# Attention passes with one row gather per tile of edges into a ring, rows copied per unit by SyncE, and a resident table of node blocks addressed by TensorE

## The reference

```python
def gatv2_layer(x, src, dst, Wl, Wr, att, bias, n_nodes, heads):
    xl = (x @ Wl).reshape(N, heads, Dh)
    xr = (x @ Wr).reshape(N, heads, Dh)
    e = leaky_relu(xl[src] + xr[dst], 0.2)
    logits = einsum('ehd,hd->eh', e, att)
    m = segment_max(logits, dst)
    a = exp(logits - m[dst])
    alpha = a / segment_sum(a, dst)[dst]
    out = segment_sum(alpha[:, :, None] * xl[src], dst)
    return out.mean(axis=1) + bias

# edges and self loops; L0 is two such layers with a relu between
x = layernorm(x + L0(x))
# L1: h = x + segment_sum(x[src], dst), then three dense layers
x = layernorm(x + L1(x))
```

## Time and profile before

| | us |
|---|---|
| runs (3) | 4044.29, 4044.32, 4049.66 |
| median | 4044.32 |
| span of the profiled execution | 4048.7 |
| layer 1 pass, first to last chunk start | about 200 to 1738 |
| layer 2 pass, first to last chunk start | 2095 to 3416 |
| TensorE busy | 3293.6 (81%) |
| VectorE busy | 2807.3 (69%) |
| GpSimd busy | 2796.9 (69%) |
| ScalarE busy | 1717.6 (42%) |

### The profile page before, as it was taken

The page is one execution under the profiler, slowest core; times in us unless marked ns, Lnnn a source line. Parts: engine busy times, 40 slices in busy tenths (PEclk is TensorE's granted clock), DMA queues, the critical chain, the costliest instruction groups (busy, mean ns, idle before and its releaser), DMA issues. The chain is left out here.

```text
span 4048.7 us, 76266 instructions
## 1 busy us (share of the span) xinstructions
PE 3293.6 (81%) x24199; PEld 2204.4 (54%) x24199; DVE 2807.3 (69%) x6887; ACT 1717.6 (42%) x3696; POOL 2796.9 (69%) x2157
## 2 busy tenths in 40 slices
PE   0399999999999999996339977777777777568986
PEld 0246666666666666674226655554455555346763
DVE  3558888888888888886537755565555555579972
ACT  3254444444444444432215433333333333147861
POOL 4488888888777777505678888888888885537630
PEclk9999999999999999986669988888888888569997
DMA  2233343343333333323114433333333332211210
GB/s 58 51 65 80 86 88 86 86 89 85 80 87 86 86 85 88 75 54 83 48 36 79 91 74 67 68 69 67 67 68 73 69 68 48 52 26 40 44 34 28
DMA packets 607173, 274.68 MB, mean 68 GB/s; under 512 B 445801, under 2 KB 568077, under 8 KB 606260
## 3 DMA queue, kind: packets, MB, share of 16 engines
q1 hardware_dynamic: 261848, 102.14, 11.7%
q0 software_dynamic: 107328, 77.78, 11.1%
q10 hardware_dynamic: 237600, 89.88, 9.1%
HBM read 161.25 MB, written 105.94 MB: 66 GB/s over the span
## 5 line engine op out<-in xcount | busy, mean ns | idle before, releaser
L901 PE MATMUL L_e_ps_z<-L_e_xT,L_w_abs 128*128 128x500 f32 x2700 | 1501.4, 642 | 0.0
L826 POOL DMA_INDIRECT L_e_xs<-in_x_dram,src_idx x880 | 1193.1, 1356 | 335.4 <-issue 261.4
L826 POOL DMA_INDIRECT L_e_xs<-x_d,src_idx x820 | 1079.7, 1317 | 253.3 <-issue 249.8
L952 PEld LDWEIGHTS L_e_ps_v<-L_e_xs,L_e_p 125*128 125x128 f32 x5400 | 860.0, 204 | 628.3 <-issue 569.6
L996 ACT ACTIVATE L_e_rl<-L_e_ps_z 128x500 f32<-128x500 f32 x1350 | 793.0, 587 | 883.0 <-PE L_e_ps_z L901 883.0
L952 PE MATMUL L_e_ps_v<-L_e_xs,L_e_p 125*128 125x65 f32 x5400 | 796.2, 274 | 11.1 <-DVE L_e_acc L1180 9.4
L1180 DVE SCALAR_TENSOR_TENSOR L_e_acc<-L_e_acc,L_e_row,L_e_ps_v 128x130 f32<-128x130 f32 (+1 forms) x1440 | 448.5, 311 | 424.1 <-PE L_e_ps_v L952 281.4
L888 PE MATMUL L_e_ps_x<-ident,L_e_xs 125*64 125x125 f32 x1800 | 288.7, 285 | 310.7 <-DMA L_e_xs<-x_d,src_idx 251.8
L989 ACT ACTIVATE L_e_xT<-L_e_ps_x 128x500 f32<-128x500 f32 x450 | 264.3, 587 | 619.3 <-PE L_e_ps_x L891 590.4
L901 PEld LDWEIGHTS L_e_ps_z<-L_e_xT,L_w_abs 128*128 128x128 f32 x2700 | 427.4, 198 | 77.8 <-issue 24.3
L1163 DVE TENSOR_TENSOR L_e_p<-L_e_ohc,L_e_ae 125x640 f32<-125x640 f32 x540 | 427.1, 818 | 0.0
(11 more groups left out here) (304 smaller groups left out, 3620.2 us busy)
## 6 DMA issues: line engine op xcount, KB each, us to landing
L_v_d<-L_e_acc ACTq DMA_DIRECT2D x225, 260.0 KB
L_e_dlb<-dloc_d SPq DMA_DIRECT2D x90, 468.8 KB, 4.9
L_v_d<-L_e_acc ACTq DMA_DIRECT2D x225, 130.0 KB
L_e_xw<-x_d SPq DMA_DIRECT2D x1800, 12.0 KB
L_e_xs<-in_x_dram,src_idx POOLq DMA_INDIRECT x900
L_e_xs<-x_d,src_idx POOLq DMA_INDIRECT x900
L_e_lim<-limits_d SPq DMA_DIRECT2D x180, 39.1 KB
L_max_d<-L_e_me SPq DMA_DIRECT2D x45, 78.1 KB
```

The source lines that it names most:

```text
L826: pool.indirect_dma_start(xs[c.slot(XR)][:, n, 0:D], None, lay.x_rows, bass.IndirectOffsetOnAxis(k.src_idx[:, u:u + 1], 0)).then_inc(gath[ ...
L901: pe.matmul(ps_z[part % ZR][:, 0:QT], lay.w_abs[:, part * 128:(part + 1) * 128], xT[q][:], start=True, stop=True).then_inc(s["z_ready"], 1)
L952: ins = pe.matmul(ps_v[u // 2 % 2][:, u % 2 * VX + v * XW:u % 2 * VX + (v + 1) * XW], p[st % 3][:, u % NQ, v, :, :].rearrange("e n h -> e ...
```

## The change

**Gathers.** GpSimd gathers each tile once (800 instead of 900 gathers a pass) into a ring `L_e_tiles` of TR = 64 tiles, in groups of TF = 16 (`fetch_tiles`). After a group has landed it adds one to `fetched_to`. Before a group is fetched over an old one, it waits until the chunks that use the old tiles are copied (`copied`, with a count read from `reuse`).

**Rows.** For each chunk SyncE runs `serve`: it waits for the chunk's list, signals `listed`, waits for the copies of the chunk before and signals `copied`, loads 20 ring places into registers with one load, waits until `fetched_to` has reached the chunk's last tile, and issues 20 copies from the ring to `L_e_xs` (now a ring of XR = 6 in both layers) inside SBUF. The list has three rows: window, place in the ring, group needed.

**Windows.** The rows of all 98 windows are loaded once per layer into SBUF. TensorE itself loads the four window addresses of the next step into registers at the end of each step (`window_blocks`) and uses them as the address of the weights. These weights are 128 columns wide, the second 64 being the window; partitions 0 to 63 of the result are overwritten by the transposes, which now come second.

**Rings.** The rings of `dlb` and of the limits have 2 places instead of 3 in layer 1. **Ahead.** Chunks served and groups fetched before the pass are 1 and 2 in layer 1, 3 and 4 in layer 2. **Setup.** Seven of nine gathers of source indices go; the indices per tile are transposed by TensorE; two more lists are stored to HBM.

The diff, cut to its core:

```diff
+TR = 64
+TF = 16
+NF = G // TF
+RF = TR // TF
+XR = 6
+LR = 8
+SERVED = (1, 3)
+FETCHED = (2, 4)
...
                 for b in range(NB):
...
+                    if b < 2:
+                        pool.indirect_dma_start(srcu[:, b * T:(b + 1) * T], None, a["src"].rearrange("(g e) -> g e", e=T),
+                                                bass.IndirectOffsetOnAxis(gidx[:, b:b + 1], 0)).then_inc(s["gather"], 16)
...
+                us = Dma(sp, s["unit_store"])
+                sp.wait_ge(s["units"], 4)
+                us.start(k.unit_d[1].rearrange("(b p) -> p b", p=BLK), ring_off[:], elements=True)
+                us.start(k.unit_d[2].rearrange("(b p) -> p b", p=BLK), need_i[:], elements=True)
+                us.wait()
...
-def fetch_rows(k, pool, lay, u0, u1):
-
-    for u in range(u0, u1):
-        pool.indirect_dma_start(lay.xs[u // CU][:, u % CU, 0:D], None, lay.x_rows,
-                                bass.IndirectOffsetOnAxis(k.src_idx[:, u:u + 1], 0)).then_inc(lay.gath[u // CU], 16)
...
-def load_windows(k, sp, lay, c):
-
-    for n in range(CU):
-        window = k.nc.values_load(lay.wins[c.slot(2)][0:1, n:n + 1], engines=[mybir.EngineType.SP], min_val=0, max_val=NW - 1,
-                                  skip_runtime_bounds_check_because="win_idx is the least of a count's rest and NW - 1")
-        sp.dma_start(lay.xw[c.slot(3)][:, n, :], bass.AP(k.x3_d.tensor, window * (WN * S3),
-                                                         [[D, 3 * WN], [1, D]])).then_inc(lay.ld_x[c.slot(3)], 16)
+def counts(eng, name, places):
+
+    regs = [eng.alloc_register(f"{name}{n}") for n in range(places.shape[1])]
+    eng.load(regs, places)
+    return [(eng.snap(r, donate=True, min_val=0, max_val=63) & 63) + 1 for r in regs]
+
+
+def fetch_tiles(k, pool, lay, f0, f1):
+
+    for f in range(f0, f1):
+        if f >= RF:
+            if (f - RF) % 16 == 0:
+                copies = counts(pool, f"{lay.nm}reuse{f}_", k.reuse[0:1, f - RF:min(f + 16, f1) - RF])
+            pool.wait_ge(lay.copied, copies[(f - RF) % 16])
+            pool.sem_inc(lay.freed, 1)
+        for i in range(TF):
+            g = f * TF + i
+            pool.indirect_dma_start(lay.tiles[:, g % TR * D:(g % TR + 1) * D], None, lay.x_rows,
+                                    bass.IndirectOffsetOnAxis(k.src_tile[:, g:g + 1], 0)).then_inc(lay.gath[f % RF], 16)
+            if i == 3 and f > f0:
+                tiles_there(pool, lay, f - 1)
+    tiles_there(pool, lay, f1 - 1)
+
+
+def tiles_there(pool, lay, f):
+
+    pool.wait_ge(lay.gath[f % RF], 16 * TF * (f // RF + 1))
+    pool.sem_inc(lay.fetched_to, 1)
+
+
+def list_units(k, sp, lay, c):
+
+    sp.dma_start(lay.lists[c.slot(LR)][:], bass.AP(k.unit_d.tensor, c.val(CU), [[3 * UT, 1], [UT, 3], [1, CU]])).then_inc(lay.ld_w[c.slot(2)], 16)
+
+
+def listed(eng, lay, c, row, start, step, top):
+
+    regs = [eng.alloc_register(f"{lay.nm}{row}_{c.number}_{n}") for n in range(start, CU, step)]
+    eng.load(regs, lay.lists[c.slot(LR)][0:1, row, start:CU:step])
+    return [eng.snap(r, donate=True, min_val=0, max_val=top) for r in regs]
+
+
+def rows_there(sp, lay, c):
+
+    sp.wait_ge(lay.ld_r[c.slot(XR)], c.uses(XR) * 16 * CU)
+    sp.sem_inc(lay.copied, 1)
+
+
+def load_rows(k, sp, lay, c):
+
+    places = listed(sp, lay, c, 1, 0, 1, (TR - 1) * D)
+    sp.wait_ge(lay.fetched_to, counts(sp, f"{lay.nm}need{c.number}_", lay.lists[c.slot(LR)][0:1, 2, CU - 1:CU])[0])
+    for n, at in enumerate(places):
+        sp.dma_start(lay.xs[c.slot(XR)][:, n, 0:D], lay.tiles[:, bass.ds(at, D)]).then_inc(lay.ld_r[c.slot(XR)], 16)
+
+
+def serve(k, sp, lay, c):
+
+    sp.wait_ge(lay.ld_w[c.slot(2)], c.uses(2) * 16)
+    sp.sem_inc(lay.listed, 1)
+    if c.after(1):
+        rows_there(sp, lay, c.back(1))
+    load_rows(k, sp, lay, c)
+    if c.back(-1).there():
+        list_units(k, sp, lay, c.back(-1))
...
+                sp.dma_start(lay.xw[:, 128 - D:].rearrange("r (w d) -> r w d", d=D),
+                             bass.AP(k.x3_d.tensor, 0, [[D, 3 * WN], [WN * S3, NW], [1, D]])).then_inc(lay.ld_x, 16)
+                serve(k, sp, lay, fixed(0))
...
-                fetch_rows(k, pool, lay, 0, EARLY if lay.norm else lay.ahead * CU)
+                pool.memset(lay.xw[:, 0:128 - D], 0.0).then_inc(s["ones"], 1)
...
+                fetch_tiles(k, pool, lay, 0, 2)
...
-                for c in map(fixed, range(lay.ahead, NCH)):
-                    if c.after(XR):
-                        pool.wait_ge(s["v_ready"], c.val(CU, CU * (1 - XR)))
-                    for n in range(CU):
-                        u = c.val(CU, n)
-                        pool.indirect_dma_start(xs[c.slot(XR)][:, n, 0:D], None, lay.x_rows,
-                                                bass.IndirectOffsetOnAxis(k.src_idx[:, u:u + 1], 0)).then_inc(gath[c.slot(XR)], 16)
+                fetch_tiles(k, pool, lay, lay.fetched, NF)
...
                     if c.there():
-                        if c.after(3):
-                            sp.wait_ge(s["x_ready"], c.val(NQ, -2 * NQ))
-                        if c.after(1):
-                            sp.wait_ge(ld_w[c.slot(2)], c.uses(2) * 16)
-                            load_windows(k, sp, lay, c)
-                        if c.back(-1).there():
-                            list_windows(k, sp, lay, c.back(-1))
-                        if c.after(3):
-                            sp.wait_ge(s["oht_ready"], c.val(1, -2))
+                        if c.after(lay.served):
+                            if c.after(XR):
+                                sp.wait_ge(s["v_ready"], c.val(CU, CU * (1 - XR)))
+                            serve(k, sp, lay, c)
+                        if c.after(SLACK):
+                            sp.wait_ge(s["oht_ready"], c.val(1, 1 - SLACK))
                         sp.dma_start(dlb[r][:], bass.AP(k.dloc_d.tensor, c.val(CU * T), [[0, 3 * WN], [1, CU * T]])).then_inc(ld_d[r], 16)
...
-                def turn(c, q):
+                def turn(c, q, blocks):
                     r = c.slot(XR)
                     if q == 0:
-                        pe.wait_ge(gath[r], c.uses(XR) * GB)
-                        pe.wait_ge(ld_x[c.slot(3)], c.uses(3) * 16 * CU)
+                        pe.wait_ge(ld_r[r], c.uses(XR) * GB)
                         pe.wait_ge(s["oht_ready"], c.val(1, 1))
                     if c.after(1) or q >= 2:
                         pe.wait_ge(s["xT_ready"], c.val(NQ, q - 1))
                     ps = ps_x[(c.slot(2) * NQ + q) % 2]
                     for j in range(Q):
                         n = j * NQ + q
-                        pe.transpose(ps[0:D, j * T:(j + 1) * T], xs[r][:, n, 0:D], k.ident[0:T, 0:T])
+                        pe.matmul(ps[:, j * T:(j + 1) * T], xw[:, bass.ds(blocks[j], 128)],
+                                  oht[c.slot(2)][:, n * T:(n + 1) * T], start=True, stop=True)
                     for j in range(Q):
                         n = j * NQ + q
-                        ins = pe.matmul(ps[D:128, j * T:(j + 1) * T], xw[c.slot(3)][:, n, :],
-                                        oht[c.slot(2)][:, n * T:(n + 1) * T], start=True, stop=True)
+                        ins = pe.transpose(ps[0:D, j * T:(j + 1) * T], xs[r][:, n, 0:D], k.ident[0:T, 0:T])
                     ins.then_inc(s["x_ready"], 1)
+
+                def window_blocks(c, q):
+                    if q == 0:
+                        pe.wait_ge(lay.listed, c.val(1, 1))
+                    return listed(pe, lay, c, 0, q, NQ, (NW - 1) * D)
...
+                    nc_, nq = lag(c, q, -1)
+                    if nc_.there():
+                        blocks[:] = window_blocks(nc_, nq)
+                pe.wait_ge(lay.ld_x, 16)
+                blocks[:] = window_blocks(fixed(0), 0)
...
+                for c in range(1, lay.served):
+                    serve(k, sp, lay, fixed(c))
...
-                fetch_rows(k, pool, lay, EARLY, lay.ahead * CU)
+                fetch_tiles(k, pool, lay, 2, lay.fetched)
```

More of the change, by code:

```diff
@@ L81, in __init__ @@
         self.x_node, self.x_rows, self.next_table, self.next_node = x_node, x_rows, next_table, next_node
-        self.v_d, self.max_d, self.norm, self.ahead = v_d, max_d, norm, AHEAD[1 if norm else 0]
-        self.ring = 9 if norm else 6
+        self.v_d, self.max_d, self.norm = v_d, max_d, norm
+        self.served, self.fetched = SERVED[1 if norm else 0], FETCHED[1 if norm else 0]
+        self.slack = 3 if norm else 2
 class Turn:
@@ L305, in _ @@
                 xs.wait()
+                l3.wait()
             @block.gpsimd
@@ L511, in _ @@
                 sp.wait_ge(s["dve3"], NB + 16)
-                st.start(k.win_d.rearrange("(b p) -> p b", p=BLK), k.win_idx[:], elements=True)
+                sp.wait_ge(s["units"], 11)
+                st.start(k.unit_d[0].rearrange("(b p) -> p b", p=BLK), win_off[:], elements=True)
                 st.start(k.row_d.rearrange("(w n) -> w n", n=WN), rowi[:])
@@ L754, in edge_pass @@
```

(21 more changed lines are left out.)

129 lines of the change are left out of this document (80 added, 49 removed).

## The result

The changed kernel takes 4248.98 us (median of 4 runs, 4244.38 to 4258.95) against 4046.99 for the kernel before on the same chip: a ratio of 1.050, 95% interval 1.049 to 1.052. The forecast was 3998, and the range ended at 4088. The change makes the kernel 5% slower.

The account below looks back on a forecast made before the run. TensorE was taken to bound pass 1 and GpSimd's gathers pass 2. Terms +35 (start), +45 (TensorE steps), -3 (between passes), -123 (pass 2) sum to -46 us: 4002.7 from the profiled 4048.7, 3998 on the median; range 3935 to 4088.

Parts of the forecast that it names:

- Step 6: TensorE's register load, register operations and wider weights in pass 1: 0.2 us per step, 225 times, +45 us.
- rival B: TensorE's register load and operations stand bare in every step of pass 1: 135 us instead of 45, 4088; chance 0.2.
- The lead of 0.4 to 0.5 us: Time TensorE's instruction stream runs ahead of its array at the turn, taken to hide the load and first operation.
- or 0.05 us gained: Lower bound for TensorE's step: 0.05 us gained if the new order saves a switch between 64-column positions.
- Step 3: Start of pass 1: more gathers beforehand and late dlb delay the first chunks, +37 us, +35 with the setup's -2.
- VectorE waits for dlb: Start of pass 1: dlb, issued behind SyncE's serving, makes VectorE's one-hot of chunk 1 33 us later.
- Step 1: Pass 2: 84 fewer gathers at 1.622 us save 136 us, less 13 at the end, so 123; waits on copies cost nothing.
- rival C: GpSimd's gathers get dearer beside the added row packets, 1.716 us each: +69 us, 4067; chance 0.1.
- a sign of being wrong: The prediction said it would be wrong if, among other signs, GpSimd waited on copies.
- Rival D: The ring holds GpSimd because copies are signalled late; from 2.7 us per group pass 2's gain is gone: 4121; chance 0.05.
- The end of pass 2: After the last gather: SyncE's 20 copies for the last chunk, 11 us, plus 1.8 us for the last landing.
- The smaller rings ... Nothing: Pass 1: rings of 2 instead of 3 only move loads to one chunk ahead of their use, costing nothing.

Follow-up runs that it names:

- e11: Changed kernel with TensorE loading one register per step instead of four, used by all four window matmuls (output not the reference's): 3981.16 us, ratio 0.985.
- e12: Changed kernel with TensorE's four registers loaded from numbers side by side instead of five apart (output not the reference's): 3987.30 us, ratio 0.986.
- e3: Changed kernel with TensorE's register load moved from the step's end to before the logit matmuls (reduce): 3981.81 us, ratio 0.984 to the kernel before.
- e5: e3 with SyncE issuing the load of dlb before it serves the chunk instead of behind: 3941.69 us, ratio 0.975 to the kernel before.
- e1: Changed kernel with window matmuls at one fixed address, no register loaded or computed on TensorE (output not the reference's): 3987.75 us, ratio 0.987.
- e6: e3 with tiles signalled in groups of 8 instead of 16: 3918.94 us, ratio 0.969 to the kernel before.

## Why the prediction was wrong, point by point

The two profiled spans differ by 200.6 us where the sum said -46:

| term | forecast | measured |
|---|---|---|
| start of pass 1 (to chunk 3), with the setup | +35 | +38.1 |
| pass 1 from there | +45 | +201.1 |
| between the passes | -3 | +11.1 |
| fewer gathers in pass 2 | -136 | -109.6 |
| last gather to last chunk | +13 | +59.1 |

- **Step 6, the register work of TensorE, is the step that failed**: 0.2 us per step, with 0.7 as its upper bound (the range stopped at rival B's 0.6), against 0.98 measured. The mechanism was named (rival B) with too small a price. "On SyncE a register load is 0.27 us" was read from loads of one number and carried over to a load of four that lie five apart; e11 and e12 show that 0.3 was right for one, or for four side by side. The bound was none: a load of another shape had no row. The four operations, priced at 0.32 with some 0.1 of it showing, show 0.17 in the changed kernel and nothing in e3. The Trainium skill (Runtime: NRT & Kernel Launch, Instruction fetch mechanics) gives about 200 ns per register even in bulk, for register loads from HBM; for four that is an estimate of 0.8 us by that page. The loads here are from on-chip memory: the strided one takes 0.99 at least, four adjacent 0.33, twenty adjacent 1.8, where an estimate by the page is 4. The page's figure doesn't fit them, and the measurement decides.
- The lead of 0.4 to 0.5 us was a fair reading for that place (it is 0.6 to 1.1 at the load's place in the changed kernel: loads at 849.8 and 858.0, array done at about 850.4 and 859.1). What I didn't ask is whether it is the same everywhere in the step: at reduce it is 2.2 us (e3).
- The gain allowed for the turn's new form ("or 0.05 us gained") is 0.32 us per step, 65 us over the 41 chunks. The load hid it: 201 us more in pass 1 are 266 for the load less these 65. The 266 are 1.30 us per step: 0.9 of idle time, 0.17 of bare operations, and some 0.2 that isn't split further. With the load hidden instead, the change lands at 3982, near the forecast, but by other terms.
- Step 3, the start, came out near its number: chunk 3 at 324.9 (forecast 322). The causes are in part others. Of the 38 us, 7 go with the register load (317.9 in e3), which step 3 didn't count, and 14 with dlb behind the serving (e5), to which the text gave 33; the other 17 stay when dlb comes first, and there chunk 1 waits for its rows. That the sum came out is in part luck. And "VectorE waits for dlb" was priced at the start alone, not at the end of pass 2.
- Step 1: 84 gathers fewer are worth 110 us, not 136, since one takes 1.658 us from start to start instead of 1.622: 27 us, over a third of what rival C feared. In pass 2 GpSimd did not wait on copies, as said; in pass 1 it did (355.6 us), which the text had named as a sign of being wrong, but at no cost: in e1 the rings and copies are the same and TensorE is busy for 1475 of the 1480 us. Rival D falls with the missing wait in pass 2.
- The end of pass 2 was priced as the copies of the last chunk alone, at 0.55 us each. A copy takes 0.83, and what counts is the chunk before: its copies, its dlb, and then TensorE's work on the rest of chunk 42 and on chunk 43, together 62 us (of the 57 that are left in e3, e5 takes off 12 and e6 10). Each of the two blocks between the passes ends with such a copy too: 2 x 20 x 0.28 = 11 of the 14 us missed there. That is worked out, not tried.
- "The smaller rings ... Nothing" holds for pass 1 (e1, e3).
